# A macaron block on one core: the normalised rows of seven of eight feed-forward blocks go through memory and are turned by VectorE in 32 by 32 blocks, not by TensorE

## The chip, the core and the metric

The kernel runs on one core of a Trainium2 chip. Its time is the device time of one execution in microseconds (us). The engines have queues of their own: TensorE (PE in the profile; PEld is its weight load), VectorE (DVE), ScalarE (ACT), GpSimd (POOL) and SyncE (SP), which issues nearly all transfers. Engines wait for each other only through semaphores, and each works through its own list strictly in order.

## The reference, cut to what matters

x has 4 batches of 512 tokens of 256 values in float32. Three stages follow each other; each first normalises every token's row.

```python
x = x + 0.5 * ffn(layernorm(x), Wg, Wu, Wd, Wr, temperature)
x = x + attn(layernorm(x), Wq, bq, Wk, bk, Wv, bv, Wo, bo)
x = x + 0.5 * ffn(layernorm(x), Wg, Wu, Wd, Wr, temperature)
# ffn: 8 experts; weights = golden_weights(x, Wr) gives each token a weight per expert
gate = jnp.einsum('btd,edf->betf', x, Wg)
up = jnp.einsum('btd,edf->betf', x, Wu)
h = jax.nn.silu(gate) * up
e_out = jnp.einsum('betf,efd->betd', h, Wd)
out = jnp.einsum('bte,betd->btd', weights, e_out)
# attn: 16 heads of 16 values, causal softmax
```

## The kernel before

**Blocks and chunks.** The two feed-forward stages are eight blocks q = 0 to 7: block q is batch q % 4 (512 tokens), blocks 0 to 3 the first stage, 4 to 7 the second. A block has 16 chunks, one for each expert and each half of its 256 hidden values, so there are 128 chunks n. Chunk n is made of `g` (gate) and `u` (up), two products into PSUM banks of a ring of six, each of two groups of three 128x512 matmuls (every float32 operand is split into a high and a low part, and a product is hi·hi + hi·lo + lo·hi); then `t` (ACT tanh, DVE product) and `h` (DVE), `hi` (POOL multiplies with the router's weight row `wb`, ACT takes the high part), `lo` (POOL takes the low part), and two chunks later `d` (down): 12 matmuls of 128x256 that add up in `dn`. Attention of batch b is woven between chunks of the blocks that are independent of it: `x`, `qk`, `v`, `max`, `mt`, `exp`, `pv`, `wo`. Its score products `max` (L942) and `exp` (L958) are bf16, all other matmuls float32 parts.

**The rows of a block.** PE needs a block's normalised rows with the 256 values on partitions. ACT writes them token by token (`ln`, L985, four 128x256 operations for a block) to `xn[m]`, m = 0, 1 for the halves of 256 tokens. PE turns each half with four 128x128 transposes into a PSUM bank (`xt`, L789, called at L879). ACT copies the bank to `xt_hi` (L1032), and DVE subtracts that from the bank to get `xt_lo` (L1282). Then `z` (L891) is the router's product, ACT copies it (L1038), PE turns it (`zt`, L896), DVE works out the experts' weights in eight pieces (`route`, L1153 to L1186), PE turns those (`wt`, L789), ACT copies them, SP stores them and loads each expert's row, broadcast, to `wb` (L1520, L1527). The first `hi` of the block needs `wb`, and all its `g` need `xt_hi` and `xt_lo`. A block q can be prepared as soon as its batch's x is final and block q - 2 no longer reads its `xt_hi`/`xt_lo` buffer (q % 2).

**What sets the order.** `schedule()` gives each item a target in units of chunks (constants such as `Q1`, `DOWN0`, `M0`, `PERIOD`, and one start for each block). `plan()` then places every item on its engine by those targets and by lengths written in it, and hands out the ring's banks. The result is a fixed list for each engine (`PE_ORDER` and so on); so a change of targets or items anywhere rearranges all five lists.

Of the kernel before, what the change touches and what calls it, by code (L numbers as in the profile page):

```python
# [39 lines left out]
NWP = 1  # L40

# [38 lines left out]
Q1 = 9.16  # L80
DOWN0, DOWN1 = 3.19, 0.87
M0, PERIOD = 27.78, 4.44
# [3 lines left out]
def schedule():  # L86
# [25 lines left out]
    for e in range(E):  # L112
        sg = (-9.46, -8.8, 0.67, 3.13, 5.47, 7.6, 8.85, 11.24)[e]
        sd = (-8.85, 0.32)[e] if e < NWD else down[FT * (e - NWD) + FT - 1] + 0.42
# [38 lines left out]
    for q in range(1, NBLOCK):  # L153
        start = CB * (q - 1) + {1: Q1, 2: 3.10, 4: 1.52, 5: 7.85, 6: 6.41, 7: 8.21}.get(q, 5.0)
# [8 lines left out]
        put(start + 1.4, ("ln", q, 1))  # L163
        put(start + 2.3, ("xt", q, 0))
# [188 lines left out]
def plan():  # L353
# [7 lines left out]
    def add(eng, item, *a, **k):  # L361
        if eng == FREED_BY.get(item[0]):
# [100 lines left out]
    for q in range(NBLOCK):  # L463
        k = min(q, 1) if q < BATCH else q - BATCH + 2
        for m in range(2):
            mine = "dve" if q + m == 0 else "act"
            add(mine, ("ln", q, m), 1.1 if mine == "dve" else 0.58 if q == 0 else 1.0, ("pool" if k else "dve", "newton", k, 1), holds=("xn", m),
                then=[routed(q - 1)] if q else [])
            add("pe", ("xt", q, m), 0.45, (mine, "ln", q, m), last_of[q - 2] if q > 1 else None,
                ("dve", "ln", 0, 0) if q + 1 == m else None, lets=("xn", m))  # L470
            add("act", ("xt", q, m), 0.5, ("pe", "xt", q, m))
            add("dve", ("xt", q, m), 0.6, ("act", "xt", q, m))
# [89 lines left out]
def build(nc, A, out):  # L562
    with ExitStack() as ctx:
# [55 lines left out]
        xt_hi = [sb(f"xt_hi{i}", [P, KT, T], F32R) for i in range(2)]  # L619
        xt_lo = [sb(f"xt_lo{i}", [P, KT, T], F32R) for i in range(2)]  # L620
# [42 lines left out]

        ct_hi = over("ct_hi", [P, KT, T], F32R, x2_at)
# [9 lines left out]

        wts_dram = dram("wts_rows", (NBLOCK, E, QT, P), F32)
# [31 lines left out]
        xb_done = sem("xb_done")  # L707
        wd_st = [sem(f"wd_st{i}") for i in range(NWD)]
# [74 lines left out]
        with nc.Block() as block:  # L783
            @block.tensor
            def _(pe):
# [6 lines left out]
                for it in PE_ORDER:  # L792
                    kind = it[0]
                    if kind in RING:
# [3 lines left out]
                    if kind in ("g", "u"):  # L798
# [83 lines left out]
                    if kind == "z":  # L882
# [92 lines left out]
            def _(act):  # L975
# [12 lines left out]
                for it in ACT_ORDER:  # L988
                    kind = it[0]
                    if kind in RING:  # L990
                        o, freed = rbank(it), ra_free[BANK[it]]
                    if kind in ("xt", "z", "wbp", "wt", "x", "qk", "v", "mt", "exp", "pv"):
# [626 lines left out]
```

## Time and profile before

| | |
|---|---|
| time, three runs | 736.78, 737.14, 738.84 us, median 737.14 |
| profiled execution, its own time | 736.52 us |
| span of its trace | 734.8 us |
| PE busy | 728.4 us, 99% |
| DVE, ACT, POOL busy | 468.0 (64%), 340.9 (46%), 417.5 us (57%) |
| moved by DMA | 90.47 MB, 123 GB/s over the span |

The span is the time between the first and the last instruction of the trace; the profiled execution's own time is 1.7 us above it. Busy time of an engine says how much work it has, not whether the end waits for it; that is read from waits and from the order of starts. Matmuls overlap in the trace: a row's duration reaches over the next one's start, so what a matmul takes from PE is the step from its start to the next start.

### The profile page before, as it was taken

How to read it: one execution, taken by the hardware profiler on the slowest of the kernel's cores; microseconds unless marked ns; L12 is line 12 of the kernel's file. 1: busy time of each engine (PE TensorE's matmuls, PEld its weight loads, DVE VectorE, ACT ScalarE, POOL GpSimd, SP SyncE). 2: the span in 40 equal slices, each digit the busy share in tenths (PEclk: the TensorE clock that was granted, in tenths of full speed). 3: DMA queues.
4: the chain of work that ended last, by engine and by line, in shares of the span. 5: the costliest groups of instructions: out<-in, count | busy, mean ns of one | idle time of the engine just before them, and what ended most of it. 6: DMA issues, size and time to landing. Idle time of an engine off the chain costs nothing.

```text
span 734.8 us, 13763 instructions
## 1 busy us (share of the span) xinstructions
PE 728.4 (99%) x4714; PEld 592.2 (81%) x4714; DVE 468.0 (64%) x1308; ACT 340.9 (46%) x661; POOL 417.5 (57%) x497
## 2 busy tenths in 40 slices
PE   8999999999999999999999999999999999999998
PEld 7888889877788777778778778778777778888887
DVE  6976966866567947686448657955658434563333
ACT  5447346344375543755434557445454433323222
POOL 3678384544764535845546843464564665656663
PEclk9999999999999999999999999999999999999999
DMA  9474234634243644145442333634323333214321
GB/s 290 145 247 144 76 109 132 175 117 145 74 112 116 177 127 122 59 130 147 142 136 88 120 99 115 178 110 145 104 78 95 98 106 114 74 72 136 116 95 58
DMA packets 69878, 90.47 MB, mean 123 GB/s; under 512 B 13232, under 2 KB 49456, under 8 KB 69808
## 3 DMA queue, kind: packets, MB, share of 16 engines
q1 hardware_dynamic: 67472, 89.03, 39.1%
q8 instruction: 38, 0.62, 0.4%
q10 hardware_dynamic: 2336, 0.56, 0.3%
q14 instruction: 32, 0.26, 0.1%
HBM read 72.36 MB, written 17.04 MB: 122 GB/s over the span
## 4 chain that ended last, share of the span: by engine, by line
PE 91%; DVE 5%; issue 1%; ACT 1%; DMA 0%; POOL 0%; DVEq 0%; ACTq 0%
PE ra L828 15%; PE ra L830 15%; PE ra L829 15%; PE dn L860 8%; PE dn L861 8%; PE dn L862 8%; PE ra L970 5%; PE ra L958 5%; PE ra L942 5%; PE ra L789 2%; PE ra L931 1%; PE ra L932 1%; PE ra L933 1%; PE ra L918 1%; PE ra L920 1%
## 5 line engine op out<-in xcount | busy, mean ns | idle before, releaser
L1455 POOL TENSOR_TENSOR hid<-hid,wb 128x512 f32<-128x512 f32 x124 | 161.8, 1307 | 146.5 <-DVE hid L1304 139.4
L1459 POOL TENSOR_TENSOR ht_lo<-hid,ht_hi 128x512 fp32r<-128x512 f32 x124 | 163.0, 1317 | 114.4 <-ACT ht_hi L1070 114.0
L828 PE MATMUL ra<-xt_hi,wgu_hi 128*128 128x512 f32 x508 | 216.2, 426 | 0.3 <-DVE hid_b L1304 0.3
L830 PE MATMUL ra<-xt_lo,wgu_hi 128*128 128x512 f32 x508 | 200.5, 395 | 0.0
L829 PE MATMUL ra<-xt_hi,wgu_lo 128*128 128x512 f32 x508 | 200.4, 395 | 0.0
L1296 DVE SCALAR_TENSOR_TENSOR hid<-hid,ra 128x512 f32<-128x512 f32 x125 | 85.5, 685 | 136.7 <-ACT hid L1062 135.7
L860 PE MATMUL dn<-wd,ht_hi 128*128 128x256 f32 x496 | 149.3, 301 | 0.6 <-POOL ht_lo L1459 0.6
L861 PE MATMUL dn<-wd,ht_hi 128*128 128x256 f32 x496 | 139.2, 281 | 0.0
L862 PE MATMUL dn<-wd,ht_lo 128*128 128x256 f32 x496 | 139.1, 280 | 0.0
L1070 ACT ACTIVATE ht_hi<-hid 128x512 fp32r<-128x512 f32 x124 | 77.8, 629 | 128.5 <-POOL hid L1455 103.5
L1361 DVE CUSTOM_DVE_ANT_0 junk<-ra,mask 128x128 bf16<-128x128 f32 (+3 forms) x256 | 112.5, 484 | 26.7 <-PE ra L942 26.3
L1062 ACT ACTIVATE hid<-ra 128x512 f32<-128x512 f32 x125 | 74.4, 596 | 88.0 <-PE ra L830 77.4
L830 PEld LDWEIGHTS ra<-xt_lo,wgu_hi 128*128 128x128 f32 x508 | 95.4, 188 | 23.2
L1122 ACT ACTIVATE probs<-ra 128x512 f32<-128x512 f32 x160 | 88.2, 597 | 51.6 <-PE ra L958 51.3
L828 PEld LDWEIGHTS ra<-xt_hi,wgu_hi 128*128 128x128 f32 x508 | 95.6, 188 | 18.3 <-issue 1.6
L1304 DVE TENSOR_TENSOR hid<-hid,ra 128x512 f32<-128x512 f32 x124 | 84.9, 685 | 34.2 <-PE ra L830 30.8
L829 PEld LDWEIGHTS ra<-xt_hi,wgu_lo 128*128 128x128 f32 x508 | 96.0, 189 | 13.2
L860 PEld LDWEIGHTS dn<-wd,ht_hi 128*128 128x128 f32 x496 | 93.5, 188 | 8.3 <-issue 1.2
L861 PEld LDWEIGHTS dn<-wd,ht_hi 128*128 128x128 f32 x496 | 93.6, 189 | 4.3
L862 PEld LDWEIGHTS dn<-wd,ht_lo 128*128 128x128 f32 x496 | 93.5, 189 | 0.0
L1409 POOL TENSOR_SCALAR_AFFINE_SELECT probs<-probs 128x640 f32<-128x640 f32 (+2 forms) x96 | 44.4, 496 | 17.0 <-ACT probs L1122 17.0
L942 PE MATMUL ra<-k_st,q_st 96*128 96x128 bf16 (+3 forms) x256 | 48.2, 303 | 0.2 <-DVE hid L1296 0.2
(178 smaller groups left out, 827.8 us busy)
## 6 DMA issues: line engine op xcount, KB each, us to landing
wd<-wd_parts SPq DMA_DIRECT2D x56, 512.0 KB, 3.5
wb<-wts_rows SPq DMA_DIRECT2D x63, 256.0 KB, 3.7
qk_parts<-parts SPq DMA_DIRECT2D x32, 192.0 KB, 2.3
q_st<-qk_parts SPq DMA_DIRECT2D x96, 64.0 KB, 2.3
k_st<-qk_parts SPq DMA_DIRECT2D x96, 64.0 KB, 2.3
wd_parts<-wd SPq DMA_DIRECT2D x8, 512.0 KB, 3.5
ctx_rows<-cx SPq DMA_DIRECT2D x16, 256.0 KB, 2.7
stage<-in_Wg SPq DMA_DIRECT2D x8, 256.0 KB, 4.3
```

The lines of the kernel that those rows point to most:

```text
L828: mm(b_, w_hi, xt_hi[q % 2][:, c, :], start=c == 0, stop=False)
L829: mm(b_, w_lo, xt_hi[q % 2][:, c, :], start=False, stop=False)
L830: last = mm(b_, w_hi, xt_lo[q % 2][:, c, :], start=False, stop=c == KT - 1)
L860: mm(b_, h_hi, w_hi, start=k == 0 and (i % 2 == 0 or apart), stop=False, skip_group_check=True)
L861: mm(b_, h_hi, w_lo, start=False, stop=False, skip_group_check=True)
L862: last = mm(b_, h_lo, w_hi, start=False, stop=k == CB - 1, skip_group_check=True)
L942: last = mm(o[:, c:c + (i + 1) * P], q_st[0:KROWS, G % NST, hh, i * P:(i + 1) * P], k_st[0:KROWS, G % NST, hh, 0:(i + 1) * P], start=True, ...
L1122: nc.scalar.activation(probs[:, r // PB, r % PB, :], o[:, :], ACT.Exp, scale=HD ** -0.5).then_inc(freed, 1)
L1296: nc.vector.scalar_tensor_tensor(out=tb, in0=tb, scalar=1.0, in1=rbank(("g", n))[:, :], op0=ALU.add, op1=ALU.mult).then_inc(ra_free[BANK[" ...
L1361: ins = nc.vector.tensor_tensor_reduce(out=junk[:, k % NJUNK, c:c + w], in0=o[:, c:c + w], in1=mask[:, T - w:T], scale=1.0, scalar=-3.0e38 ...
L1455: nc.gpsimd.tensor_tensor(tb, tb, wb[m % NWB][:, :], ALU.mult).then_inc(hw_done, 1)
L1459: nc.gpsimd.tensor_tensor(ht_lo[n % NHT][:, :], hidden(n)[:, :], f32(ht_hi[n % NHT][:, :]), ALU.subtract).then_inc(lo_done, 1)
```

## The change

For blocks 1 to 7 (`MOVED = 1`) the eight PE transposes of a block go. In their place:

- ACT's `ln` writes `xn[m]` in another order of values, so that pieces of 128 values lie together.
- SP stores each half with four transfers (`xst`, 64 KB each, from 32 partitions, runs of 128 values) and loads it back with two (`xld`, 128 KB each) into `xt_hi`, after the stores have landed and after block q - 2 has read that buffer. The 32 by 32 blocks then lie in their places, each still to be turned in itself.
- DVE turns them with four 128x128 operations a half (`turn`) into `xt_raw`, which lies where `xt_lo` lies.
- ACT copies `xt_raw` to `xt_hi`, DVE subtracts: `xt_lo = xt_raw - xt_hi`, now from SBUF and not from PSUM.
- A later use of `xn[m]` waits for the stores' semaphore instead of PE's.
- 14 PSUM bank turns fall away, and the targets of `schedule()` are set anew.

```diff
+MOVED = 1
-Q1 = 9.16
-DOWN0, DOWN1 = 3.19, 0.87
-M0, PERIOD = 27.78, 4.44
+Q1 = 6.91
+DOWN0, DOWN1 = 3.08, 0.89
+M0, PERIOD = 27.80, 4.38
...
+        for m in range(2 if q >= MOVED else 0):
+            put(start + 1.3 + 0.2 * m, ("xst", q, m))
+            put(start + 1.7 + 0.2 * m, ("xld", q, m))
+            put(start + 2.1 + 0.4 * m, ("turn", q, m))
...
+            if q >= MOVED:
+                add("sp", ("xst", q, m), 1.7, (mine, "ln", q, m), lets=("xn", m), kb=256)
+                add("sp", ("xld", q, m), 0.9, ("sp", "xst", q, m), last_of[q - 2] if q > 1 else None, kb=256)
+                add("dve", ("turn", q, m), 0.7, ("sp", "xld", q, m))
...
+        xt_raw = [over(f"xt_raw{i}", [P, KT, T], F32, lo_at + 4096 * i) for i in range(2)]
+        xn_dram = dram("xn_blocks", (NBLOCK, 2, QT, QT, 32, 4 * 32), F32)
...
-                            pe.wait_ge(*emptied(("xt", q, 0)))
-                            pe.wait_ge(*emptied(("xt", q, 1)))
+                            pe.wait_ge(*rows_low(q, 0))
+                            pe.wait_ge(*rows_low(q, 1))
...
+                        if q >= MOVED:
+                            nc.vector.tensor_tensor(xt_lo[q % 2][:, :, half], xt_raw[q % 2][:, :, half],
+                                                    f32(xt_hi[q % 2][:, :, half]), ALU.subtract).then_inc(lo_turned, 1)
...
+                    if kind == "turn":
+                        dve.wait_ge(xn_ld[m], 32 * (q - MOVED + 1))
+                        for i in range(2):
+                            for c in range(KT):
+                                blocks = f32(xt_hi[q % 2][:, :, half]).rearrange("p a (b i c f) -> p i c a b f", b=2, i=2, c=KT)
+                                rows = xt_raw[q % 2][:, c, half].rearrange("p (i w f) -> p i w f", i=2, w=QT)
+                                ins = nc.vector.transpose(rows[:, i, :, :].rearrange("p (a b) f -> p a b f", a=2),
+                                                          blocks[:, i, c, :, :, :])
+                        ins.then_inc(turned, 1)
...
+                    if kind == "xst":
+                        sp.wait_ge(ln_done, 2 * (2 * q + m) - 1)
+                        for w in range(QT):
+                            sp.dma_start(xn_dram[q, m, w].rearrange("v a k -> a v k"),
+                                         rows[32 * w:32 * (w + 1), :, :]).then_inc(xn_st[m], 16)
+                    if kind == "xld":
+                        sp.wait_ge(xn_st[m], 64 * (q - MOVED + 1))
+                        if q > 1:
+                            sp.wait_ge(gu_full, 2 * CB * (q - 1))
+                        for a in range(2):
+                            sp.dma_start(f32(xt_hi[q % 2][:, a, m * HT:(m + 1) * HT]).rearrange("p (b k) -> p b k", b=2),
+                                         xn_dram[q, m, 2 * a:2 * a + 2].rearrange("b v a k -> (v a) b k")).then_inc(xn_ld[m], 16)
```

**Three places in the order.** PE, before, the preparation of block 7 inside chunk 107 (L828 to L830 are a group of three of `g` or `u`, L789 the transposes of one half):

```order
L828 MATMUL ra<-xt_hi,wgu_hi 128x512
L829 MATMUL ra<-xt_hi,wgu_lo 128x512
L830 MATMUL ra<-xt_lo,wgu_hi 128x512
L789 MATMUL ra<-ident,xn 128x128 x4
L828 MATMUL ra<-xt_hi,wgu_hi 128x512
L829 MATMUL ra<-xt_hi,wgu_lo 128x512
L830 MATMUL ra<-xt_lo,wgu_hi 128x512
L789 MATMUL ra<-ident,xn 128x128 x4
L828 MATMUL ra<-xt_hi,wgu_hi 128x512
L829 MATMUL ra<-xt_hi,wgu_lo 128x512
L830 MATMUL ra<-xt_lo,wgu_hi 128x512
```

PE, of the change, where block 7's router product `z` (L918) and its turn `zt` (L923) now stand, in chunk 109 (L855 to L857 are what L828 to L830 were, L887 to L889 are `d`):

```order
L855 MATMUL ra<-xt_hi,wgu_hi 128x512
L856 MATMUL ra<-xt_hi,wgu_lo 128x512
L857 MATMUL ra<-xt_lo,wgu_hi 128x512
L918 MATMUL ra<-xt_hi,wr 72x512 x2
L918 MATMUL ra<-xt_lo,wr 72x512 x2
L855 MATMUL ra<-xt_hi,wgu_hi 128x512
L856 MATMUL ra<-xt_hi,wgu_lo 128x512
L857 MATMUL ra<-xt_lo,wgu_hi 128x512
L887 MATMUL dn<-wd,ht_hi 128x256
L888 MATMUL dn<-wd,ht_hi 128x256
L889 MATMUL dn<-wd,ht_lo 128x256
L923 MATMUL ra<-ident,xn 128x72 x4
```

The transposes are gone, and `z` has moved from behind `d` of chunk 105 into `u` of chunk 109; `wo` of the last batch, from which this chain starts, has moved from behind `u` of chunk 104 to behind `g` of chunk 103. Between `wt` and `d` of chunk 112 there stood, before, the last two quarters of `d` 109 and work up to `g` 115; now there stand, in order, 3 groups of three of `g` and `u`, 8 quarters of `d` and 8 groups of three.

DVE, of the change, the same preparation (L1349 is `t`, L1357 `h`, L1334 `turn`, L1321 the subtraction to `xt_lo`):

```order
L1357 TENSOR_TENSOR hid<-hid,ra 128x512
L1334 STREAM_TRANSPOSE xt_raw_50<-xt_hi 128x128 x4
L1349 SCALAR_TENSOR_TENSOR hid<-hid,ra 128x512
L1334 STREAM_TRANSPOSE xt_raw_50<-xt_hi 128x128 x4
L1321 TENSOR_TENSOR xt_lo<-xt_raw_50,xt_hi 128x2x256
L1357 TENSOR_TENSOR hid<-hid,ra 128x512
L1321 TENSOR_TENSOR xt_lo<-xt_raw_50,xt_hi 128x2x256
```

Before, the two subtractions stood together between `t` and `h` of chunk 107; now two turns that wait for transfers stand in front of `t` and `h` of chunk 108.

SP, of the change, the same stretch (L1583 loads an expert's down weights, L1595 an expert's `wb`, L1542 is `xst`, L1550 `xld`):

```order
L1583 DMA wd<-wd_parts 128x1024
L1542 DMA xn_blocks<-xn 32x4x128 x8
L1595 DMA wb<-wts_rows 128x512
L1550 DMA xt_hi<-xn_blocks 128x2x128 x4
L1583 DMA wd<-wd_parts 128x1024
L1595 DMA wb<-wts_rows 128x512
```

Before, only the weight loads stood here, in turns of L1515 and L1527; now a store that waits for `ln` and a load that waits for the store stand between them.

## Rows read from the trace of the kernel before

**Rows 1.** The page, part 1: busy time of each engine.
```profile
PE 728.4 (99%) x4714; PEld 592.2 (81%) x4714; DVE 468.0 (64%) x1308; ACT 340.9 (46%) x661; POOL 417.5 (57%) x497
```

**Rows 2.** Waits of PE from 9 us on: total, times, longest.
```profile
PE dn L860 <- POOL ht_lo L1459: 0.6, 1, 0.6
...
PE ra L942 <- DVE hid L1296: 0.2, 1, 0.2
```

**Rows 3.** Timeline of PE, 209 to 214 us: start, duration, instruction.
```profile
209.99 0.60 PE L789 MATMUL ra<-ident,xn 128*128 128x128 f32 x4
210.35 0.48 PE L828 MATMUL ra<-xt_hi,wgu_hi 128*128 128x512 f32 x1
210.66 0.40 PE L829 MATMUL ra<-xt_hi,wgu_lo 128*128 128x512 f32 x1
210.90 0.40 PE L830 MATMUL ra<-xt_lo,wgu_hi 128*128 128x512 f32 x1
...
212.64 1.04 PE L789 MATMUL ra<-ident,xn 128*128 128x128 f32 x8
213.43 0.36 PE L860 MATMUL dn<-wd,ht_hi 128*128 128x256 f32 x1
213.63 0.28 PE L861 MATMUL dn<-wd,ht_hi 128*128 128x256 f32 x1
```

**Rows 4.** Timeline of PE, 202 us: float32 matmuls right behind a bf16 product.
```profile
202.15 0.47 PE L860 MATMUL dn<-wd,ht_hi 128*128 128x256 f32 x1
202.46 0.28 PE L861 MATMUL dn<-wd,ht_hi 128*128 128x256 f32 x1
202.57 0.28 PE L862 MATMUL dn<-wd,ht_lo 128*128 128x256 f32 x1
```

**Rows 5.** Timeline of ACT at 637 us: `ln` of block 7.
```profile
637.00 2.08 ACT L985 ACTIVATE xn<-x_res,shift,rstd 128x256 f32<-128x256 f32 x4 [0.74 <-POOL shift L1427]
```

**Rows 6.** Timeline of SP at 634 us: one issue.
```profile
633.79 0.32 SPq L1515 DMA_DIRECT2D wd<-wd_parts  x1
```

**Rows 7.** The page, part 6: DMA issues, KB of each, us from issue to landing.
```profile
q_st<-qk_parts SPq DMA_DIRECT2D x96, 64.0 KB, 2.3
...
ctx_rows<-cx SPq DMA_DIRECT2D x16, 256.0 KB, 2.7
...
x_res<-in_x SPq DMA_DIRECT2D x3, 512.0 KB, 8.7
```

**Rows 8.** Timeline of DVE, 641 to 658 us: preparing block 7.
```profile
641.57 0.69 DVE L1282 TENSOR_TENSOR xt_lo<-ra,xt_hi 128x512 fp32r<-128x512 f32 x1 [0.29 <-ACT xt_hi L1032]
...
645.63 0.23 DVE L1286 TENSOR_REDUCE z<-ra 128x32 f32<-128x64 f32 x1 [2.78 <-PE ra L896]
...
657.19 0.22 DVE L1186 SCALAR_TENSOR_TENSOR wts<-zone,sums 128x32 f32<-128x32 f32 x1
```

**Rows 9.** Groups of DVE by line and shape: count, busy us, mean ns, idle before.
```profile
L1361 DVE CUSTOM_DVE_ANT_0 junk<-ra,mask 128x128 bf16<-128x128 f32 x64 | 18.0, 282 | 9.2 <-PE ra L942 8.9
...
L1244 DVE TENSOR_TENSOR wd<-stage,wd 128x512 fp32r<-128x512 f32 x8 | 8.0, 1000 | 0.9 <-ACT wd L1009 0.9
```

**Rows 10.** Timeline of PE: `z` and `wt` of block 7, `d` of chunk 112.
```profile
642.86 0.62 PE L891 MATMUL ra<-xt_hi,wr 128*72 128x512 f32 x2
...
661.62 0.27 PE L789 MATMUL ra<-ident,wts 128*32 128x128 f32 x1
...
672.96 0.28 PE L860 MATMUL dn<-wd,ht_hi 128*128 128x256 f32 x1
```

**Rows 11.** Timeline of POOL: `lo` of chunk 0, and of 112 and 113.
```profile
26.37 2.31 POOL L1459 TENSOR_TENSOR ht_lo<-hid_a,ht_hi 128x512 fp32r<-128x512 f32 x1
...
28.63 1.31 POOL L1459 TENSOR_TENSOR ht_lo<-hid_b,ht_hi 128x512 fp32r<-128x512 f32 x1
...
671.18 2.55 POOL L1459 TENSOR_TENSOR ht_lo<-hid,ht_hi 128x512 fp32r<-128x512 f32 x2
```

**Rows 12.** Timeline of PE at 29 us: `d` of chunk 0.
```profile
29.32 0.28 PE L860 MATMUL dn<-wd,ht_hi 128*128 128x256 f32 x1
```

More of the change, by code:

```diff
@@ L112, in schedule @@
     for e in range(E):
-        sg = (-9.46, -8.8, 0.67, 3.13, 5.47, 7.6, 8.85, 11.24)[e]
-        sd = (-8.85, 0.32)[e] if e < NWD else down[FT * (e - NWD) + FT - 1] + 0.42
+        sg = (-9.46, -8.8, 0.56, 3.13, 5.26, 7.31, 8.85, 11.09)[e]
+        sd = (-8.85, 0.57)[e] if e < NWD else down[FT * (e - NWD) + FT - 1] + 0.42
         put(sg, ("sg", e))
@@ L361, in add @@
     def add(eng, item, *a, **k):
-        if eng == FREED_BY.get(item[0]):
+        if eng == FREED_BY.get(item[0]) and not (item[0] == "xt" and item[1] >= MOVED):
             k["frees"] = item
@@ L707, in build @@
         xb_done = sem("xb_done")
+        xn_st = [sem(f"xn_st{m}") for m in range(2)]
+        xn_ld = [sem(f"xn_ld{m}") for m in range(2)]
+        turned = sem("turned")
+        lo_turned = sem("lo_turned")
         wd_st = [sem(f"wd_st{i}") for i in range(NWD)]
@@ L761, in emptied, with xn_read, rows_low @@
             return ra_free[BANK[it]], TURN[it] + 1
+        def xn_read(it):
+            if it[0] == "xt" and it[1] >= MOVED:
+                return xn_st[it[2]], 64 * (it[1] - MOVED + 1)
+            return ra_full, full(it)
+        def rows_low(q, m):
+            return (lo_turned, 2 * (q - MOVED) + m + 1) if q >= MOVED else emptied(("xt", q, m))
         def hidden(n):
@@ L793, in _ @@
                     kind = it[0]
-                    if kind in RING:
+                    if kind in RING and it in BANK:
                         o = rbank(it)
@@ L989, in _ @@
                     kind = it[0]
-                    if kind in RING:
+                    if kind in RING and it in BANK:
                         o, freed = rbank(it), ra_free[BANK[it]]
-                    if kind in ("xt", "z", "wbp", "wt", "x", "qk", "v", "mt", "exp", "pv"):
+                    if kind in ("xt", "z", "wbp", "wt", "x", "qk", "v", "mt", "exp", "pv") and it in BANK:
                         act.wait_ge(ra_full, full(it))
@@ L1025, in _ @@
                         if it in XN_BEFORE:
-                            act.wait_ge(ra_full, full(XN_BEFORE[it]))
+                            act.wait_ge(*xn_read(XN_BEFORE[it]))
                         for i in range(1 if it == ("ln", 0, 1) else 0, 2):
-                            ins = normalise(xn[m][:, i, :], b * QT + 2 * m + i)
+                            if kind == "ln" and it[1] >= MOVED:
+                                dst = xn[m][:, :, :].rearrange("p j d -> p (j d)").rearrange(
+                                    "p (w i c f) -> p w i c f", w=QT, i=2, c=KT)[:, :, i, :, :]
+                                t = b * QT + 2 * m + i
+                                ins = nc.scalar.activation(dst, x_res[:, t, :].rearrange("p (c w f) -> p w c f", c=KT, w=QT),
+                                                           ACT.Identity, scale=rstd[:, t:t + 1], bias=shift[:, t:t + 1])
+                            else:
+                                ins = normalise(xn[m][:, i, :], b * QT + 2 * m + i)
                             ins.then_inc(ln_done if kind == "ln" else aln_done, 1)
@@ L1031, in _ @@
                         q, m = it[1:]
-                        nc.scalar.activation(xt_hi[q % 2][:, :, m * HT:(m + 1) * HT],
-                                             o[:, :].rearrange("p (c t) -> p c t", c=KT),
-                                             ACT.Copy).then_inc(xhi_done, 1)
+                        half = slice(m * HT, (m + 1) * HT)
+                        if q >= MOVED:
+                            act.wait_ge(turned, 2 * (q - MOVED) + m + 1)
+                            rows = xt_raw[q % 2][:, :, half]
+                        else:
+                            rows = o[:, :].rearrange("p (c t) -> p c t", c=KT)
+                        nc.scalar.activation(xt_hi[q % 2][:, :, half], rows, ACT.Copy).then_inc(xhi_done, 1)
                     if kind == "z":
                         if it in XN_BEFORE:
-                            act.wait_ge(ra_full, full(XN_BEFORE[it]))
+                            act.wait_ge(*xn_read(XN_BEFORE[it]))
                         nc.scalar.activation(z_rows[0:ZC, :], o[0:ZC, :], ACT.Copy).then_inc(freed, 1)
@@ L1191, in _ @@
                     kind = it[0]
-                    if kind in RING:
+                    if kind in RING and it in BANK:
                         o, freed = rbank(it), ra_free[BANK[it]]
```

29 lines of the change are left out of this document (19 added, 10 removed).

## The prediction

> **What bounds the kernel now.** I read the busy line of the page first: PE is busy 728.4 of 734.8 us [rows 1], and the other engines no more than two thirds. A busy share alone doesn't say that PE sets the time, so the waits come next: from 9 us on, when it has its first inputs, PE waits four times, between 0.6 and 0.2 us each, 1.4 us in all [rows 2]. The other 5 us in which PE is idle are the first loads and what follows its last matmul. Whatever is taken out of PE's list comes off the time in full, if nothing newly waits; whatever is added to DVE, ACT, POOL or SP costs nothing until PE waits for it.
>
> **What is removed.** 56 transposes, in 14 halves of four. A matmul's duration overlaps the next one's, so their price is read from starts. One half: from its start at 209.99 to the second product behind it at 210.66 there are 0.67 us, of which one product's own step, 0.24 (210.66 to 210.90), has to be left: 0.43 us. Two halves together: 212.64 to 213.63 is 0.99, less a down step of 0.12: 0.87 us, or 0.44 each [rows 3, 4]. 14 x 0.435 = **6.1 us**. Their banks are given back too, but PE hardly waited for banks, so that is worth nothing by itself.
>
> **What the new order adds to PE.** A float32 matmul right behind a bf16 score product takes 0.31 us to the next start (202.15 to 202.46) where others take 0.12 (202.46 to 202.57) [rows 4]: 0.19 us a switch. PE's list left a bf16 product for another kind 149 times before and 153 times now (counted in both lists): 4 x 0.19 = **0.8 us** back. Everything else on PE is the same work.
>
> **What is added elsewhere.** DVE gets 56 operations of 128x128. No such operation is in the trace; the nearest row by size is the 128x128 piece of the maximum, 282 ns, and the far ends are 0.2 us (a 128x32 router operation, 0.22 in the row at 657.19) and 0.69 us (a 128x512 one, at 641.57) [rows 8, 9]. I take 0.28, so 1.1 us a half and 16 us in all, 11 and 39 us at the ends. The 14 subtractions now have both inputs in SBUF. The row of the same shape with two SBUF inputs (L1244) has a mean of 1.00 us, against 0.69 with one in PSUM [rows 8, 9]: 14 x 0.31 = 4 us. DVE rises from 468 to 488 us, far from full. Both are priced at nothing as long as `t` and `h` behind them in DVE's list stay ahead of PE.
>
> That row also bears on a rule. The Trainium skill, SBUF — State Buffer, section "Who interferes with whom", says that a VectorE instruction with two SBUF inputs contends with a GpSimd one that reads SBUF, and one of them blocks for the whole instruction; by that rule each moved subtraction may stand a whole POOL operation longer, 18 us on DVE in place of 4, which is still under PE's list and leaves the sum as it is. By that rule the trace agrees: L1244 is longer, though by only 0.31 us on the mean.
>
> SP gets 8 stores of 64 KB and 4 loads of 128 KB a block, 7.3 MB in all on 90.5. What matters is latency. A half's store is four issues of 0.32 us, the last of which lands 2.3 us after its start, 3.3 us; its load is two issues and, between the rows for 64 and 256 KB, 2.3 to 2.7 us: 3.0 us [rows 6, 7]. The far bound of such a leg is 8.7 us, what three 512 KB loads took in the crowded start [rows 7].
>
> **The chain of a block, on block 7,** which has the least room. It starts with `wo` of batch 3 and goes by DVE's sums and POOL's Newton steps to `ln`, which ends at 639.1 [rows 5]. Before: the rows were ready at 642.26 [rows 8], 3.2 us later. Now: 3.3 + 3.0 + 1.1 (turn) + 0.6 (ACT's copy; the four of half that size in [rows 5] take 0.52 each) + 0.9 (DVE's subtraction) = 8.9 us, so 5.7 more, and up to 7.5 with a `t` or `h` (0.7 each) ahead of them on DVE. Against that stands the order. A `g`, a `u` or a `d` is 1.4 us of PE (six products of 0.235 or twelve of 0.12). `z`, at 642.86 before [rows 10], has moved past `g` and `u` 108, `d` 106, `g` 109 and half of `u` 109, 6.3 us, less the 0.9 of the transposes; `wo` has come forward past `u` 103, `d` 101, `g` and `u` 104, 5.6 us. So there are 11 us more of PE's work for a chain that is 5.7 to 7.5 longer: no wait, 3 to 5 us spare.
>
> Then `z` to the weights. From the reduction of `z` to the last routing operation it took 11.8 us [rows 8], `t` and `h` in between included. From `zt` to `wt` PE now has three quarters of a `d` and nine items of 1.4 us, 13.7 us: enough. From `wt` (661.62) to `d` 112 (672.96) took 11.34 us, and the `lo` that it waits for ended at 671.18 + 2.55 / 2 = 672.46, so with a semaphore 10.9 us were needed [rows 10, 11]. The new list has 11 groups of three (0.70 each), 8 quarters of `d` (0.35) and `wt` itself (0.1) there: 10.6 us. **PE waits 0.3 us** at `d` 112.
>
> **Chunk 0.** The new `DOWN0` puts `d` 0 and 1 in front of `g` 5, 2.1 us of PE's work earlier. `lo` 0 ended at 28.68, and PE came at 29.32 [rows 11, 12], so if nothing else changed PE would wait 1.4 us. But that `lo` took 2.31 us where others take 1.3, beside a two-input operation of DVE that the new list has elsewhere; I take half, 0.7 us, bounds 0 and 1.5. The earlier statistics (`Q1`) also crowd DVE in the first 60 us. I add 0.5 us for all waits of PE that I can't place (before it had 1.4, and I let these stay).
>
> **Sum.** 736.5 - 6.1 + 0.8 + 0.3 + 0.7 + 0.5 = 732.7 us for an execution like the profiled one. That one stood 0.6 us under the median of its three; I take half of this for a median's habit and say **733.0 us**. Its own range is 730.7 (neither new waits nor a price for the switches) to 734.8. A measurement of this kernel can tell some 0.3%, 2.2 us, from no change.
>
> **Rivals.**
> 1. *Waits eat the gain (no change told).* DVE stands at a turn until the load lands, with `t` and `h` behind it. For: two of its items a block now hang on two transfers one after the other, and an in-order SP queue in which `xst` waits for ACT. Against: 3 to 5 us spare in block 7, and 8.7 us or more of PE work from `z` to its block's first `g` in every block. From 14 x 0.3 us of waits on, the result is within 0.3%: with 4 us of them the time is about 737. Chance 0.14.
> 2. *The transfers' latency turns into PE's time (slower).* From about 5 us a leg on, in place of 3.2, a block's two legs use up the spare 4 us, and it decides from some 10 us of such waits on. At the bound of 8.7 us a leg the chain is 11 us longer, less 4, so 7 us a block where the room is as in block 7; for blocks 1 and 7, which have least PE work between `z` and their first `g`, that is 14 us, about 746. For: no row shows a store from 32 partitions only. Against: 96 loads of 64 KB for `q_st` take 2.3 us in the midst of all other traffic [rows 7]. Chance 0.06. The Trainium skill speaks against the change here: VectorE: DVE Perf Modes, section "The three transpose paths", calls plain copies that transpose by access-pattern strides 19 times slower than the transposing transfer. By that rule this rival is the likely one; but in the lists the transfers move whole runs of 128 values and VectorE turns inside the blocks, so I give it no more than this.
> 3. *The turns are slow.* At 0.69 us each a half takes 2.8 us, 39 us on DVE, 70% busy. The chain is 3.4 us longer, within the spare; `t` and `h` come up to 2.8 us late 14 times, where PE has a bank or two in hand. I price it at 0.2 us a half, 3 us: 736. Inside rival 1's chance.
> 4. *More than the sum.* If waits vanish, 6.1 - 0.8 and old waits of 1.4: 729.8. Chance 0.03.
>
> **How the numbers follow.** The likeliest case has 0.77. Rival 1 ends at 735 to 739; most of it is near its lower end. The range to hold eight in ten is 730.6 to 736.0: it takes in the sum with all its bounds and a third of rival 1. Faster by over 0.3% (below 734.9) is the likeliest case and rival 4, 0.80; within 0.3% is rival 1, 0.13 of its 0.14; the rest of it and rival 2 are slower, 0.07.
>
> **What the new profile should show.** PE busy near 723, its L816 row for `xn` with 40 and not 96. A step of 0.44 us for each half gone. STREAM_TRANSPOSE at 0.2 to 0.4 us, 56 of them; the subtraction L1321 at about 1.0. `xn_blocks` 2.3 us and `xt_hi` 2.3 to 2.7 us to landing. PE waits 2 to 3.5 us in all, the largest at `d` of chunk 0 or 112, behind POOL's `lo`. I am wrong if PE waits for `xt_hi`, `xt_lo` or a bank that DVE empties after a turn, or if PE's steps between other products have grown.

## The result, and the profile after

The changed kernel takes 732.40 us (median of 6 runs, 731.47 to 734.84) against 737.64 us for the kernel before beside it (6 runs): a ratio of 0.9933, 95% interval 0.9912 to 0.9954. That is the gain forecast, and the forecast time of 733.0 us is 0.6 us off.

The page of the changed kernel, part 1, answers to [rows 1]:

```profile
PE 723.0 (99%) x4658; PEld 587.6 (80%) x4658; DVE 476.0 (65%) x1364; ACT 342.3 (47%) x661; POOL 420.4 (58%) x497
```

Its two largest waits of PE from 9 us on (us in total, times, longest), of 2.6 us in all, against [rows 2]:

```profile
PE ra L923 <- ACT xn L1076: 1.1, 2, 0.8
PE ra L855 <- ACT wb L1094: 0.6, 1, 0.6
...
```

The span is 730.7 us, 4.1 less than before. The two views say where they come from: PE is busy 5.4 us less (728.4 to 723.0), and its waits have grown by 1.2 us (1.4 to 2.6). The transposes are gone and nothing has taken their place. The largest new wait is 1.1 us at `zt` (L923), which stands behind ACT's copy of `z`; the 0.6 us at L855 come early in the kernel, and the kernel with the new targets and all its transposes (targets_only, below) has them too.

What was added, and what is left of PE's transposes of `xn` (40, where there were 96), by line and shape (group, count, busy us, mean ns, idle before), against [rows 9]:

```profile
L1321 DVE TENSOR_TENSOR xt_lo<-xt_raw,xt_hi 128x512 fp32r<-128x512 f32 x14 | 13.1, 944 | 1.7 <-ACT xt_hi L1072 1.7
L1334 DVE STREAM_TRANSPOSE xt_raw<-xt_hi 128x128 f32<-128x128 f32 x56 | 12.3, 277 | 3.3 <-DMA xt_hi<-xn_blocks 3.3
...
L816 PE MATMUL ra<-ident,xn 128*128 128x128 f32 x40 | 5.9, 274 | 0.2 <-DVE xn L1263 0.2
```

and the new transfers, as in [rows 7] (KB each, us from issue to landing):

```profile
xn_blocks<-xn SPq DMA_DIRECT2D x56, 64.0 KB, 1.8
xt_hi<-xn_blocks SPq DMA_DIRECT2D x28, 128.0 KB, 3.2
```

Block 7, for which the prediction had worked out the room (block 4 has still less, 0.4 us): timelines of PE (`wo`, where the chain starts), ACT, SP, DVE and PE (start, duration, instruction, idle before it and what ended that), against [rows 5, 6, 8, 10].

```profile
614.93 0.36 PE L958 MATMUL ra<-wa,ct_hi 128*128 128x256 f32 x1 [0.21 <-DVE ct_lo L1435]
...
629.75 2.08 ACT L1059 ACTIVATE xn<-x_res,shift,rstd 128x256 f32<-128x256 f32 x4 [0.89 <-POOL shift L1480]
...
630.87 3.92 SPq L1542 DMA_DIRECT2D xn_blocks<-xn  x8
634.89 0.38 SPq L1595 DMA_DIRECT2D wb<-wts_rows  x1
635.37 1.93 SPq L1550 DMA_DIRECT2D xt_hi<-xn_blocks  x4
...
640.33 0.89 DVE L1334 STREAM_TRANSPOSE xt_raw<-xt_hi 128x128 f32<-128x128 f32 x4 [2.10 <-DMA xt_hi<-xn_blocks]
...
643.68 0.68 DVE L1321 TENSOR_TENSOR xt_lo<-xt_raw,xt_hi 128x512 fp32r<-128x512 f32 x1
...
644.46 0.63 PE L918 MATMUL ra<-xt_hi,wr 128*72 128x512 f32 x2
644.92 0.62 PE L918 MATMUL ra<-xt_lo,wr 128*72 128x512 f32 x2
...
646.87 0.44 PE L923 MATMUL ra<-ident,xn 72*128 72x72 f32 x4 [0.27 <-ACT xn L1076]
```

To be read as one chain. `ln` ends at 629.75 + 2.08 = 631.83. SP spends 3.92 us on the eight stores of both halves (0.49 us an issue, not 0.32), has a `wb` load in between, and issues the first load of rows at 635.37. DVE stands until the rows are there, at 640.33. The rows are ready at 643.68 + 0.68 = 644.36, 12.5 us after `ln`, and PE comes for the low part at 644.92. Its two products on the high part, at 644.46, need ACT's copies alone, the last of which ended at 643.25. So PE doesn't wait, but only by 0.6 us.

Two parts of the chain are longer than a look at the stores shows. The first load of rows lands late: the second of the first half's two loads, issued at 635.81, has the row

```profile
xt_hi<-xn_blocks SPq DMA_DIRECT2D x1, 128.0 KB, 4.5
```

where the median of all 28 is 3.2 us. And the way from `wo` to the end of `ln` has grown as well. In the kernel before, `wo` of the last batch starts at

```profile
625.15 0.28 PE L931 MATMUL ra<-wa,ct_hi 128*128 128x256 f32 x1
```

and `ln` ends at 639.08, 13.9 us later; now it is 614.93 to 631.83, 16.9 us.

### The profile page after: what moved, and what is told of

Read it like the earlier page. It is cut to its first block, busy times and chain, and to the rows that moved or that the text cites. A ratio compares the mean times of both kernels' runs of the same rounds, so it can differ in the third digit from the quotient of the medians.

```text
span 730.7 us, 13792 instructions
## 1 busy us (share of the span) xinstructions
PE 723.0 (99%) x4658; PEld 587.6 (80%) x4658; DVE 476.0 (65%) x1364; ACT 342.3 (47%) x661; POOL 420.4 (58%) x497
## 4 chain that ended last, share of the span: by engine, by line
PE 89%; DVE 4%; DMA 2%; POOL 2%; issue 1%; SPq 1%; ACT 1%; ACTq 0%; DVEq 0%; POOLq 0%
PE ra L855 15%; PE ra L857 14%; PE ra L856 14%; PE dn L887 7%; PE dn L888 7%; PE dn L889 7%; PE ra L997 5%; PE ra L969 5%; PE ra L985 5%; PE ra L958 1%; PE ra L945 1%; PE ra L960 1%; PE ra L959 1%; PE ra L946 1%; PE ra L947 1%
## 5 line engine op out<-in xcount | busy, mean ns | idle before, releaser
L1508 POOL TENSOR_TENSOR hid<-hid,wb 128x512 f32<-128x512 f32 x124 | 165.5, 1337 | 156.9 <-DVE hid L1357 144.5
L855 PE MATMUL ra<-xt_hi,wgu_hi 128*128 128x512 f32 x508 | 214.7, 423 | 0.6 <-ACT wb L1094 0.6
L857 PE MATMUL ra<-xt_lo,wgu_hi 128*128 128x512 f32 x508 | 200.7, 395 | 0.0
L1349 DVE SCALAR_TENSOR_TENSOR hid<-hid,ra 128x512 f32<-128x512 f32 x125 | 85.4, 684 | 122.5 <-ACT hid L1100 121.9
L887 PE MATMUL dn<-wd,ht_hi 128*128 128x256 f32 x496 | 150.2, 303 | 0.1
L889 PE MATMUL dn<-wd,ht_lo 128*128 128x256 f32 x496 | 139.0, 280 | 0.0
L857 PEld LDWEIGHTS ra<-xt_lo,wgu_hi 128*128 128x128 f32 x508 | 95.4, 188 | 23.1
L855 PEld LDWEIGHTS ra<-xt_hi,wgu_hi 128*128 128x128 f32 x508 | 95.6, 188 | 18.3 <-issue 0.9
L1357 DVE TENSOR_TENSOR hid<-hid,ra 128x512 f32<-128x512 f32 x124 | 84.8, 684 | 25.3 <-PE ra L857 21.7
L887 PEld LDWEIGHTS dn<-wd,ht_hi 128*128 128x128 f32 x496 | 93.5, 188 | 7.5 <-issue 1.0
L889 PEld LDWEIGHTS dn<-wd,ht_lo 128*128 128x128 f32 x496 | 93.5, 189 | 0.0
L985 PE MATMUL ra<-q_st,k_st 98*128 98x512 bf16 (+3 forms) x256 | 48.4, 303 | 0.0
```

What stands on the lines that cost most here:

```text
L855: mm(b_, w_hi, xt_hi[q % 2][:, c, :], start=c == 0, stop=False)
L857: last = mm(b_, w_hi, xt_lo[q % 2][:, c, :], start=False, stop=c == KT - 1)
L887: mm(b_, h_hi, w_hi, start=k == 0 and (i % 2 == 0 or apart), stop=False, skip_group_check=True)
L889: last = mm(b_, h_lo, w_hi, start=False, stop=k == CB - 1, skip_group_check=True)
L985: last = mm(o[:, c:c + T - j * P], k_st[0:SROWS, G % NST, hh, j * P:(j + 1) * P], q_st[0:SROWS, G % NST, hh, j * P:T], start=True, stop=True)
L1349: nc.vector.scalar_tensor_tensor(out=tb, in0=tb, scalar=1.0, in1=rbank(("g", n))[:, :], op0=ALU.add, op1=ALU.mult).then_inc(ra_free[BANK[" ...
```

## The experiments

All times are medians of runs on one chip beside runs of the kernel before, and ratios are to those. The theory to be tested: **the gain is PE's own time for 56 transposes, and the new targets only make the room in which the longer chain of the rows is hidden.** Rivals: the targets alone bring the gain; the freed banks or vanished waits do; the added transfers or DVE's turns cost part of it again. PE's busy time includes the matmuls of the first 10.1 us, ahead of the first `g`, which take between 7.3 and 8.3 us from trace to trace; where a difference of a microsecond matters, they are left out.

**targets_only.** `MOVED = 8`, so every block is turned by PE as before, with the new targets.

```diff
-MOVED = 1
+MOVED = 8
```

> The change's targets with no block moved (MOVED = 8): all 96 transposes stay on TensorE. Theory A, the gain is the 56 transposes' own 0.11 us steps on a TensorE that never waits: 736.5 to 738.5 us, no gain, ratio to before 0.998 to 1.003. Rival B, the gain comes from the targets set anew: near 732.4 us, ratio 0.993.

736.84 us (12 runs), ratio 0.9996, 0.9985 to 1.0007. PE busy in this kernel:

```profile
PE 728.1 (99%) x4714; PEld 593.8 (81%) x4714; DVE 470.4 (64%) x1308; ACT 341.9 (46%) x661; POOL 419.0 (57%) x497
```

The targets alone bring nothing. With the same targets and the transposes gone PE is busy 5.1 us less (728.1 to 723.0), and 5.7 us less from 10.1 us on (720.4 to 714.8).

**change_old_targets.** The change, with before's numbers in `schedule()`.

```diff
-Q1 = 6.91
+Q1 = 9.16
...
-    start = CB * (q - 1) + {1: Q1, 2: 2.76, ...
+    start = CB * (q - 1) + {1: Q1, 2: 3.10, ...
```

> The change with the targets of before. Theory A: TensorE's busy time is 5 to 6 us shorter; waits for rows that arrive later take 0 to 3 us of it: 731.5 to 735 us. Rival B (targets make the gain): 737 us. A result above 735 with TensorE waiting at z or at a block's first gate says that the new targets are what makes room for the longer chain.

750.83 us (4 runs), ratio 1.0185, 1.0163 to 1.0208: slower than before by 13.7 us, and far outside the 731.5 to 735 us of my theory; it is the last case of the expectation, in which the new targets make the room. The four largest waits of PE, of 14.5 us in all:

```profile
PE ra L855 <- DVE xt_lo L1321: 4.7, 1, 4.7
PE ra L918 <- ACT xt_hi L1072: 3.4, 1, 3.4
PE dn L887 <- POOL ht_lo L1512: 2.3, 2, 1.9
PE ra L923 <- ACT xn L1076: 2.0, 1, 2.0
```

and the two stretches of a low clock at the first two (window, us, then busy us and count of PE, PEld, DVE, ACT, POOL, the granted clock as a share of the full one, DMA share, GB/s):

```profile
80.50:87.20 6.70, 4.47 (x11) 3.16 (x12) 2.13 (x2) 0.59 (x1) 1.58 (x1) 0.50 0.05 21
104.40:114.50 10.10, 6.90 (x24) 5.23 (x25) 3.80 (x8) 5.84 (x12) 9.20 (x18) 0.50 0.35 91
```

PE waits for block 1's rows at 78 to 82.7 us. From 80.5 to 87.2 us the granted clock is 0.50, the lower of its two levels (1.2 of 2.4 GHz), and a 128x512 product takes 0.43 us to the next start (83.29 to 83.72) where it takes 0.24 at the full clock (90.56 to 90.80). The same comes again around the waits at block 2's `z` and `zt`, from 104.4 to 114.5 us. PE is busy 11.4 us in the two stretches; at 0.43 in place of 0.24, which is an estimate from one product, some 5 us of that are the clock's. Sum: the span is 747.8 us, 17.1 above the change's; 11.9 of it are waits (14.5 less 2.6), 5.3 are PE's longer busy time, 728.3 against 723.0.

**one_target, two_targets.** As change_old_targets, with block 1's start new (`Q1 = 6.91`), and with block 1's and block 2's (2.76) new.

> As two_targets, but block 2's start is before's too (3.10), so that only block 1's start is new. My theory: the wait at block 1's g is gone with the slow stretch behind it (about 4.7 us of waiting and 3 us of clock), block 2's z still waits 3 to 4 us with a slow stretch behind it: 738 to 745 us. Rival: block 1's delay is what makes block 2 late too; then it is as fast as two_targets, at 732 to 736 us.

> The change with all of before's targets except two: block 1's start (Q1 = 6.91) and block 2's start (2.76) are the new ones. My theory: the 13 us that the change loses with the old targets come from these two preparations, whose rows are not ready when PE comes (block 1's g and block 2's z), and from the lower clock behind those waits. Then this kernel is at 732 to 736 us, PE waits under 4 us in all and no wait over 1 us at block 1's g or block 2's z; what is left of 1.9 us of waiting for ht_lo after 640 may stay. Rival: the period of attention (M0, PERIOD, head) makes the room; then it stays above 743 us.

737.43 us (10 runs), ratio 1.0005, 0.9996 to 1.0014, and 735.83 us (10 runs), ratio 0.9990, 0.9981 to 0.9999. Here my theory for one_target fell and its rival's mechanism held: with block 1 alone started earlier the wait at block 2's `z` is gone too, although its time ended above the range the rival gave. For two_targets the time fell into the range of my theory (732 to 736 us) and far below its rival's 743; but PE waits 5.2 us in all, where I had said under 4. The largest wait is nearly the same in both (two_targets shown):

```profile
PE dn L887 <- POOL ht_lo L1512: 3.1, 4, 1.8
```

So one number, the start of block 1, decides over 1.8% or 13 us (ratios 1.0185 and 1.0005); block 2's start brings about 1 us, which is barely clear of the noise, and the other targets together (`DOWN0`, experts' loads, blocks 4, 5 and 7, attention's period) another 3 to 4, of which the waits above for `lo` are the part that I can name.

**moved_from_4.** Four of seven blocks by memory, 32 of 56 transposes gone.

```diff
-MOVED = 1
+MOVED = 4
```

> MOVED = 4: only blocks 4 to 7 go through memory, 32 of the 56 transposes. Theory A: the gain goes with the number of transposes, 32/56 of 6.1 us is 3.5 us, less waits and switches: 733.5 to 735.5 us. Rival B: 732.4 us, as with all moved. Rival C, the gain sits in the crowded start (block 1 to 3): 737 us.

735.05 us (8 runs), ratio 0.9972, 0.9958 to 0.9986; PE busy 725.4 us. The gain grows with the transposes taken away: none, 32 and 56 of them give ratios of 0.9996, 0.9972 and 0.9933, and PE busy 728.1, 725.4 and 723.0.

**transposes_back.** The change, with eight transposes of the identity put ahead of each `z` of blocks 1 to 7, in `z`'s bank, so that PE has its old work back and nothing else is altered.

```diff
+                        if q >= MOVED:
+                            for j in range(8):
+                                transpose(o[:, j % 4 * P:(j % 4 + 1) * P], ident[:, :])
```

> The change, with eight transposes of the identity put in front of z of blocks 1 to 7, into z's own bank, which z then overwrites: the work on TensorE is back, the memory path stays. Theory A: + 56 x 0.11 = 6.1 us, 738 to 739 us. Rival D, that the freed banks or the shorter wait for ScalarE and VectorE copies give the gain: no more than 2 us above 732.4.

736.65 us (12 runs), ratio 0.9994, 0.9984 to 1.0003. Timeline of PE at one of the seven places:

```profile
648.34 1.03 PE L816 MATMUL ra<-ident 128*128 128x128 f32 x8
649.13 0.71 PE L921 MATMUL ra<-xt_hi,wr 128*72 128x512 f32 x2
649.68 0.62 PE L921 MATMUL ra<-xt_lo,wr 128*72 128x512 f32 x2
```

Eight transposes take 0.79 us to the next start, and the two products behind them 0.55 instead of 0.46 (644.46 to 644.92 above): 0.88 us, as predicted from [rows 3] (0.87). Seven times that is 6.1, but the median rose by 4.3 (an expected 738 to 739 us was missed by over 1) and PE busy by 4.5. The busy time is low by 0.9 us of the start; the first 10.1 us of the change and of this kernel have

```profile
0.00:10.10 10.10, 8.25 (x46) 7.82 (x46) 5.42 (x26) 3.62 (x5) 3.03 (x12) 1.00 0.77 237
0.00:10.10 10.10, 7.31 (x46) 6.88 (x46) 5.47 (x26) 3.57 (x6) 3.03 (x12) 1.00 0.75 235
```

so from there on PE is busy 5.5 us more (714.8 to 720.2), and it waits 1.1 us less there (2.5 to 1.4), for the waits at `zt` are gone. That ACT and DVE catch up while PE turns is my reading of this, not tested. Some 0.6 us of the 6.1 I can't place. The work put back thus takes 4.3 of the 5.2 us away, with the freed banks, transfers and turns all as in the change, which rules out that those bring the gain (rival D had no more than 2 us).

**turns_twice.** Each half's turns made twice, behind each other.

```diff
-                        for i in range(2):
+                        for k, i in enumerate((0, 1, 0, 1)):
+                            if k == 2:
+                                ins.then_inc(again, 1)
+                                dve.wait_ge(again, 2 * (q - MOVED) + m + 1)
```

> The change with each half's four turns made twice, one set after the other: 56 more operations of 0.27 us on DVE, 15 us in all, PE's work unchanged. My theory: DVE's busy time costs nothing by itself; only the 1.1 to 2.2 us that the rows come later count, in blocks 4, 7, and a little in 1 and 5: 0.5 to 4 us of PE waits, 733 to 737 us. Rival: DVE's added work is what the gain is cut by, so that twice of it takes at least as much as the change gained (5 us): 737 us or more, with PE waiting for t, h or a bank in many chunks.

739.41 us (6 runs), ratio 1.0035, 1.0023 to 1.0048; span 736.7, 6.0 above the change's. My theory falls, by number and by place, and its rival (737 us or more) holds. DVE's busy time rose by 12.1 us (476.0 to 488.1), and the waits of PE by 5: only some 2 of these are at `z` and `zt` of blocks 4 and 7, the rest is behind DVE in general. The largest waits of PE:

```profile
PE ra L924 <- ACT xn L1077: 1.6, 2, 1.0
PE dn L888 <- POOL ht_lo L1516: 1.5, 1, 1.5
PE ra L919 <- DVE xt_lo L1322: 1.0, 2, 0.5
```

and the timelines of DVE and PE at 86 us:

```profile
86.04 3.51 DVE L1338 STREAM_TRANSPOSE xt_raw<-xt_hi 128x128 f32<-128x128 f32 x16
89.47 0.65 DVE L1353 SCALAR_TENSOR_TENSOR hid<-hid,ra 128x512 f32<-128x512 f32 x1
...
92.13 0.39 PE L888 MATMUL dn<-wd,ht_hi 128*128 128x256 f32 x1 [1.46 <-POOL ht_lo L1516]
```

A `t` (L1353) stands behind 3.5 us of turns, its `hi` and `lo` on POOL come that much later, and `d` waits. An engine that is busy two thirds of the span has stretches in which it isn't free. Rival 1 of the prediction is this mechanism; the change stays just short of it.

**stores_twice.** Each half's four stores issued twice, the first time into an array that nobody reads.

```diff
+                        for to in (xn_more, xn_dram):
                             for w in range(QT):
-                                sp.dma_start(xn_dram[q, m, w]...
+                                sp.dma_start(to[q, m, w]...
```

> The change with every store of the rows made twice, first into a second array that nobody reads, then into the one that is loaded: four more issues of SP a half, some 0.49 us each, so the rows of a block are ready up to 3.9 us later. Nothing is added to PE. The spare between the rows' end and z, read from the changed kernel's trace, is 1.4, 16, 31, 0.4, 1.3, 4.3 and 0.6 us in blocks 1 to 7. My theory: PE waits at z in blocks 1, 4, 5 and 7, 2.5 to 3.5 us each, 9 to 13 us together with no other waits, plus a lower clock behind each: 741 to 753 us. Rival, my prediction's own account of block 7, 3 to 5 us spare and more in every other block: under 2 us of waits, 732 to 735 us.

754.65 us (4 runs), ratio 1.0246, 1.0222 to 1.0271. Its largest waits of PE, of some 18 us in all:

```profile
PE dn L888 <- POOL ht_lo L1513: 5.2, 4, 3.2
PE ra L919 <- ACT xt_hi L1073: 2.9, 1, 2.9
```

DVE's wait for the load, from 50 us on, and the window behind PE's longest wait (columns as above):

```profile
DVE xt_raw L1335 <- DMA xt_hi<-xn_blocks: 25.3, 8, 6.3
```

```profile
65.80:69.10 3.30, 3.30 (x14) 2.91 (x13) 2.59 (x6) 2.13 (x5) 1.70 (x2) 0.50 1.01 363
```

The time is 1.7 us above the range that I had given (741 to 753). The direction and block 7 (2.9 + 0.5 us at `z`, expected 2.5 to 3.5) came as expected, while all waits at `z` are 5.0 us and not 9 to 13, and the prediction's account of 3 to 5 us of spare is refuted: it would have hidden this. But the larger part is elsewhere. DVE stands 25.3 us at the turns, against 3.3 in the change, with `t`, `h` and attention's `max` behind it, and PE then waits for `lo` or a bank (`mx`, 2.4 us at the longest). PE is busy 9.4 us more. The granted clock is 0.50 in three stretches of some 3.3 us, behind waits of 3.2, 1.4 and 2.9 us (from 65.8, 318.4 and 669.9 us on), in which PE is busy 9.7 us; by the same estimate as above some 4 us of the 9.4 are the clock's, and the rest I can't place. These waits are rivals 1 and 2 of the prediction, brought about on purpose by 3.9 us of issues a block.

**stores_shared, shared_old_targets.** The second half's stores issued by ACT behind `ln`, to shorten the chain; with the new and with the old targets.

```diff
+                        if kind == "ln" and m == 1 and it[1] >= MOVED:
+                            act.wait_ge(ln_done, 4 * it[1] + 1)
+                            for w in range(QT):
+                                act.dma_start(xn_dram[it[1], 1, w]...).then_inc(xn_st[1], 16)
...
-                        for w in range(QT):
+                        for w in range(0 if m else QT):
```

> The change, but the second half's four stores are issued by ACT right behind ln and not by SP, so that the halves' stores no longer stand behind each other in SP's list. Theory: in the changed kernel SP spends eight issues of 0.49 us a block on the stores before it comes to the first load; with four of them elsewhere the rows are ready 1 to 2 us earlier in the blocks whose chain sets it (1, 4, 5, 7), z's room in block 7 grows from 0.6 to some 2 us, and of PE's 2.6 us of waits 1 to 1.5 go: 730.5 to 732.5 us, against 732.4 for the change. Rival: ACT stands some 2 us for the four issues with tanh behind them, and PE waits for ACT or DVE in its place: 733 to 735 us.

> The same sharing of the stores, with before's targets. If it is the length of the chain by which the old targets lose (a wait of 4.7 us at block 1's first g, 3.4 us at block 2's z and a lower clock behind each), 1 to 2 us less of it a block take at least a third of the loss over the change with new targets (18 us) away: 738 to 746 us, with the wait at block 1's g at 2 to 3.5 us. If the loss has to do with the order and not with the chain's length, it stays at 749 to 752 us.

744.19 us (5 runs), ratio 1.0094, 1.0076 to 1.0111, and 757.58 us (4 runs), ratio 1.0283, 1.0268 to 1.0299. Both theories missed. Timelines of ACT and SP of stores_shared in block 7:

```profile
639.54 2.08 ACT L1059 ACTIVATE xn<-x_res,shift,rstd 128x256 f32<-128x256 f32 x4 [0.90 <-POOL shift L1486]
641.65 2.18 ACTq L1068 DMA_DIRECT2D xn_blocks<-xn  x4
643.93 0.60 ACT L1106 ACTIVATE hid<-ra 128x512 f32<-128x512 f32 x1 [2.31 <-issue]
...
640.66 1.83 SPq L1548 DMA_DIRECT2D xn_blocks<-xn  x4
644.73 3.67 SPq L1556 DMA_DIRECT2D xt_hi<-xn_blocks  x4
```

and what SP itself waits for between 640 and 650 us:

```profile
SPq L1556 <- DMA xn_blocks<-xn: 3.2, 2, 1.8
```

From the end of `ln` (641.62) to the first load's issue are 3.1 us, against 3.5 in the change, because the load also waits for the stores' landing. The four load issues reach over 3.67 us, against 1.93, because SP stands 1.8 us between the halves until ACT's stores have landed; a half's two issues take 0.9 us in all. ACT stands 2.3 us for its issues, tanh behind it. So hardly anything is won, and PE waits in a dozen places, up to 1.8 us each: 9.9 us against 2.6. That is the rival's mechanism, at more than its price. Whether the chain's length alone explains the old targets' loss this pair can't tell, as it hardly shortened the chain: the wait at block 1's first `g` is 4.7 us as before.

**strided_load_7.** Block 7 alone by memory, stored row by row (two transfers a half, from all 128 partitions, and not four from 32) and loaded with strides that transpose, without any turn.

```diff
+                            sp.dma_start(xt_raw[q % 2][:, c, m * HT:(m + 1) * HT],
+                                         xn_dram[q, m, :, :, c * P:(c + 1) * P].rearrange("i t p -> p (i t)"), ...
```

> Only block 7's rows go through memory (MOVED = 7, targets of the change), and nobody turns them: each half is stored row by row in two transfers, and each of two loads transposes by its strides, so that every 4-byte value is a piece of its own (131,072 pieces a block in place of 2,048 runs of 512 B). The Trainium skill's rule on copies that transpose by access-pattern strides (VectorE: DVE Perf Modes, section The three transpose paths) would make these loads some 19 times slower than a transposing transfer. Without a row of my own I bound it by this case's: the load of 128 KB in runs of 512 B lands after 3.2 us; were it 19 times that, 61 us a load, block 7's z waits 60 to 120 us and the time is 800 to 860 us. Rival: the number of pieces hardly matters beside the bytes, the loads land within 5 us, and the time is that of a change of block 7 alone, 735 to 740 us.

One run, 807.89 us beside a median of 736.48 for the kernel before. The DMA issues (KB, us to landing) have the first of its four loads with

```profile
xt_raw<-xn_blocks SPq DMA_DIRECT2D x1, 128.0 KB, 21.6
```

the timeline of SP their first two issues and the load of `wd` behind all four,

```profile
638.19 0.37 SPq L1537 DMA_DIRECT2D xt_raw<-xn_blocks  x1
638.61 19.46 SPq L1537 DMA_DIRECT2D xt_raw<-xn_blocks  x1
...
695.91 19.17 SPq L1571 DMA_DIRECT2D wd<-wd_parts  x1
```

and the waits of PE

```profile
PE ra L918 <- ACT xt_hi L1072: 70.1, 1, 70.1
```

The first load lands after 21.6 us instead of 3.2, 6.8 times as long. Its issue takes 0.37 us; each issue behind it, of the three other strided loads (19.46, 18.30 and 19.30 us) and of the plain `wd` load, holds SP for 18 to 19.5 us. The median of the four is 40.5 us, as the later loads stand behind the one before. One block costs 71 us. The time fell into the range that I had given, but not for its reason: I had 61 us a load, and what fills the 70 us is that four loads of some 20 us follow each other. The expectation also set 131,072 pieces against 2,048 runs of 512 B; those are a block's stores and loads together, the loads alone are 1,024. The Trainium skill's rule, VectorE: DVE Perf Modes, section "The three transpose paths", is borne out in kind only: its 19 is against the transposing transfer, which no run here has, and for large strides on the side that is written, where here they are on the side that is read. The change keeps clear of it by moving runs of 128 values.

## Why the prediction was right, and what in it was not

**Right, with its size.** The bound (PE, which hardly waits) and the price of the transposes. 6.1 us less and 0.8 us for the bf16 switches make 5.3; PE busy fell by 5.4. targets_only, moved_from_4 and transposes_back show that the gain goes with the transposes; the price of eight, 0.87, was measured again at 0.88. The 0.8 for the switches was not tested alone, but both traces can be counted through from 10.1 us on: they have the 149 and 153 switches, and the steps of the float32 matmuls behind them lie 19.9 and 21.2 us in sum above the median step of their kind. So a switch takes 0.13 to 0.14 us on the mean and not 0.19, and the change pays 1.3 us in sum and not 0.8. That the two terms together come within 0.1 us of the measured 5.4 is thus in part chance.

**Right in sum by luck, wrong in place: the new waits.** I had 0.3 us at `d` 112, 0.7 at chunk 0 and 0.5 unplaced, 1.5 in all; measured are 1.2 more, and neither place has one. `d` 112 starts at 671.52, and the `lo` that it needs ended at 670.24. At chunk 0 the step that failed is the `lo` that takes 2.31 us: the timelines of POOL and PE of the changed kernel have

```profile
25.86 1.30 POOL L1512 TENSOR_TENSOR ht_lo<-hid_a,ht_hi 128x512 fp32r<-128x512 f32 x1
...
27.56 0.28 PE L887 MATMUL dn<-wd,ht_hi 128*128 128x256 f32 x1
668.95 2.57 POOL L1512 TENSOR_TENSOR ht_lo<-hid,ht_hi 128x512 fp32r<-128x512 f32 x2
```

so without its slow neighbour it took 1.30 and was in time (27.16 for 27.56). The waits that did come are 1.1 us at `zt`, in two blocks together, which I had not looked at: there PE has too little work between `z` and its turn, 1.2 us in block 7 and 2.0 in block 4. That 1.5 us which did not come where I had put them and 1.2 us elsewhere are nearly equal is chance.

**Wrong: "no wait, 3 to 5 us spare" in block 7.** There was no wait, but 0.6 us of room, and in block 4, which I had not counted, 0.4. PE's part was near: from the start of `wo` to `z` 29.5 us pass now and 17.7 did before, 11.8 us more, where I had 11. The step that failed is the length of the chain, 12.3 us more where I had 5.7 to 7.5. Of this 3.0 us lie ahead of `ln`, where I had counted nothing: from `wo` to the end of `ln` it took 13.9 us and takes 16.9. The rest lies behind it, 12.5 us and not 8.9. From `ln`'s end to the first load's issue it is 3.5 us instead of 3.3, and the reason differs from mine: the eight stores of both halves stand in one queue at 0.49 us each, a `wb` load among them, where I had costed one half with issues of 0.32 us from [rows 6]. The load takes 4.9 instead of 3.0 (its second transfer lands after 4.5 us), and turn, copy and subtraction 4.0 instead of 2.6, with `t` and `h` in between. stores_twice shows what that room was worth. I had counted no gain on the spare, so its loss took nothing from the sum; but that a chain 5 to 7 us longer than costed still ended before PE came, by half a microsecond in two blocks, is luck, and with it that rival 1 did not come true.

**Wrong: added DVE work "costs nothing".** It was nearly true of the 8 us that were added net (468.0 to 476.0; I had 20, in part because I added up turns that overlap: four take 0.89 us and not 1.1). turns_twice shows the next 12 us at a cost of 6 to 7. "Far from full" was a reading of the mean, not of the stretches.

**Terms that were near.** A turn 0.28 us, measured 0.277. The subtraction 1.00, measured 0.944 on the mean; but that is ten of 0.65 to 0.69 and four of 1.39 to 1.78, so the mean was right and no single one takes it. The store's landing 2.3, measured 1.8; the load's 2.3 to 2.7, measured 3.2 in the median and up to 4.8.

**Said too little.** The prediction took the new targets as a list to count in, and did not ask what the change would be without them. They are what the gain depends on: 18 us between the two versions.

## What to carry to other kernels

Where, as here, the first engine hardly ever waits, its own instructions are the gain, and their price is the step to the next start; work handed to others is free only while the chain that it lengthens still ends before the first engine comes. So give the longer chain its head start first, and count each issue of a shared queue, at its own measured length, for all halves that go through it. Ask for the room in every stretch of the helping engine, not for its mean.

## What was not expected of the hardware

- During waits of PE of 4.7 and of 3.4 us (with 2.0 more close behind the second) the granted clock fell to 0.50 and stood there for 6.7 and 10.1 us in change_old_targets; in stores_twice it did so for some 3.3 us each behind waits of 3.2, 1.4 and 2.9 us. PE was busy 5.3 and 9.4 us longer in these kernels than in the change; the clock accounts for most of the first and for less than half of the second.
- Store issues from 32 partitions took SP 0.46 to 0.49 us each from start to start (3.92 for eight), load issues of rows 0.48, where the load of `wd` takes 0.32. On ACT they took 0.54 each (2.18 for four), during which ACT did nothing else.
- The first issue of a strided load of 32,768 pieces took SP 0.37 us, and each issue behind one, even that of a plain `wd` load, 18 to 19.5 us.
- The four long ones of the 14 subtractions (0.65 to 1.78 us, median 0.69) lie beside two-input operations of POOL. Timelines of DVE and POOL of the changed kernel:

```profile
449.94 1.77 DVE L1321 TENSOR_TENSOR xt_lo<-xt_raw,xt_hi 128x512 fp32r<-128x512 f32 x1
...
449.77 1.39 POOL L1508 TENSOR_TENSOR hid<-hid,wb 128x512 f32<-128x512 f32 x1 [2.29 <-DVE hid L1357]
...
643.84 1.68 POOL L1508 TENSOR_TENSOR hid<-hid,wb 128x512 f32<-128x512 f32 x1 [2.14 <-DVE hid L1357]
```

  POOL's ends at 451.16 and DVE's 0.55 later, as if it had hardly begun before. The other three long ones, too, end 0.54 to 0.55 us behind the end of a POOL operation that had started first. At 643.84 DVE was first (643.68 to 644.36, above), and POOL's operation took 1.68 in place of 1.3. The prediction weighed the Trainium skill's rule for this, SBUF — State Buffer, section "Who interferes with whom", from a mean of 1.00 us; by that rule, with the whole instruction blocked, DVE's would end some 0.65 us behind POOL's, and these rows agree to 0.1 us.
